# Moving statistics, sums and loads between engines in a 64-graph two-layer GNN kernel

## The reference

```
h = relu(layernorm(x))
q, k, v = h @ Wq.T + bq, h @ Wk.T + bk, h @ Wv.T + bv
p = adj * exp(q @ k.T)
x1 = x + (p / p.sum(axis=2)) @ v                       # layer 0
h1 = relu(layernorm(x1))
hat = adj + eye;  s = hat.sum(-1) ** -0.5
out = x1 + (hat * s[:, None] * s[None, :]) @ (h1 @ W + b)   # layer 1
```

## Time and profile before

| | before |
|---|---|
| median of 3 runs | 1765.69 us (1755.89 to 1776.26) |
| the profiled execution | 1769.79 us |
| its span in the trace | 1768.0 us |
| TensorE busy | 94% |
| VectorE busy | 90% |
| GpSimd busy | 56% |
| ScalarE busy | 49% |
| granted TensorE clock, mean | 0.991 |

### The profile page before, as it was taken

The page is one execution under the profiler, slowest core; times in us unless marked ns, Lnnn a source line. Parts: engine busy times, 40 slices in busy tenths (PEclk is TensorE's granted clock), DMA queues, the critical chain, the costliest instruction groups (busy, mean ns, idle before and its releaser), DMA issues.

```text
span 1768.0 us, 37337 instructions
## 1 busy us (share of the span) xinstructions
PE 1661.1 (94%) x12010; PEld 1558.4 (88%) x12010; DVE 1583.7 (90%) x3558; ACT 866.5 (49%) x1875; POOL 985.6 (56%) x970
## 2 busy tenths in 40 slices
PE   8899999999999999999999999999999999999997
PEld 6789899898888888899998888988998988998996
DVE  6889999999989989899999989989999999998995
ACT  3545445454544454454454454445544444554542
POOL 2655555556556556556556555555665655665561
PEclk9999999999999999999999999999999999999998
DMA  5454354354454554544544543544544545545530
GB/s 174 102 118 132 91 148 131 91 143 126 102 139 112 119 137 98 136 134 102 135 133 100 137 133 90 146 120 105 142 123 106 139 110 121 139 114 118 139 97 27
DMA packets 494415, 212.66 MB, mean 120 GB/s; under 512 B 402496, under 2 KB 427072, under 8 KB 494400
## 3 DMA queue, kind: packets, MB, share of 16 engines
q1 hardware_dynamic: 492480, 210.89, 47.2%
q10 hardware_dynamic: 1920, 1.58, 0.3%
HBM read 146.28 MB, written 66.13 MB: 120 GB/s over the span
## 4 chain that ended last, share of the span: by engine, by line
DVE 29%; issue 29%; POOL 24%; ACT 14%; PE 3%; POOLq 1%; DMA 1%; ACTq 0%; DVEq 0%; SPq 0%
DVE late L740 7%; POOL hat L313 5%; POOL hat_hi L312 5%; POOL hat_lo L315 5%; POOL ht_sum_lo L300 4%; DVE ht L638 4%; ACT late L430 4%; ACT h_hi L432 4%; DVE z_lo L734 3%; DVE st_x L615 3%; POOL rs L318 2%; ACT ht_hi L478 2%; ACT ht_sum_hi L401 2%; DVE p L747 2%; POOL xb L333 1%
## 5 line engine op out<-in xcount | busy, mean ns | idle before, releaser
L333 POOL TENSOR_TENSOR xb<-xb,bv_row 128x512 f32<-128x512 f32 x128 | 165.8, 1316 | 292.3 <-DMA xb<-in_x_dram 292.3
L300 POOL TENSOR_TENSOR ht_sum_lo<-ht_sum,ht_sum_hi 128x512 fp32r<-128x512 f32 x128 | 194.2, 1537 | 207.6 <-ACT ht_sum_hi L401 207.5
L797 PE MATMUL ps<-ht_hi,m_hi 128*128 128x256 f32 x1024 | 286.2, 279 | 0.6 <-DVE m_lo L523 0.6
L799 PE MATMUL ps<-ht_lo,m_hi 128*128 128x256 f32 x1024 | 285.8, 279 | 0.0
L800 PE MATMUL ps<-ht_hi,m_lo 128*128 128x256 f32 x1024 | 285.6, 279 | 0.0
L797 PE MATMUL ps<-w_hi,z_hi 128*128 128x512 f32 x512 | 209.0, 408 | 50.9 <-DVE z_lo L734 50.8
L406 ACT ACTIVATE g_hi<-ps,u_col 128x256 fp32r<-128x256 f32 x256 | 106.2, 466 | 203.9 <-PE ps L800 203.9
L800 PE MATMUL ps<-w_hi,z_lo 128*128 128x512 f32 x512 | 204.6, 400 | 0.0
L799 PE MATMUL ps<-w_lo,z_hi 128*128 128x512 f32 x512 | 204.3, 399 | 0.0
L797 PEld LDWEIGHTS ps<-ht_hi,m_hi 128*128 128x128 f32 x1024 | 192.5, 188 | 0.7 <-DVE m_lo L523 0.7
L800 PEld LDWEIGHTS ps<-ht_hi,m_lo 128*128 128x128 f32 x1024 | 192.4, 188 | 0.0
(11 more groups left out here) (146 smaller groups left out, 5773.4 us busy)
## 6 DMA issues: line engine op xcount, KB each, us to landing
x_in<-in_x_dram SPq DMA_DIRECT2D x64, 512.0 KB, 6.7
xb<-in_x_dram SPq DMA_DIRECT2D x64, 512.0 KB, 7.4
out_dram<-late SPq DMA_DIRECT2D x128, 256.0 KB, 2.1
h_scratch<-h SPq DMA_DIRECT2D x62, 512.0 KB, 3.8
h_blocks<-h_scratch SPq DMA_DIRECT2D x248, 128.0 KB, 4.8
adj_in<-in_adj_dram SPq DMA_DIRECT2D x64, 256.0 KB, 2.9
adj_blocks<-in_adj_dram SPq DMA_DIRECT2D x256, 64.0 KB, 2.5
dn_row<-dn_scratch SPq DMA_DIRECT2D x64, 128.0 KB, 2.9
```

Source lines behind the costliest of these rows:

```text
L300: pool.tensor_tensor(ht_sum_lo[:, pair], ht_sum[:, pair], ht_sum_hi[:, pair].bitcast(fp32), ALU.subtract).then_inc(ht_sum_lo_ready, 1)
L333: last = pool.tensor_tensor(xb[:, t, :], xb[:, t, :], bv_row[:], ALU.add)
L797: pe.matmul(dst, a_hi[:, c, cols], b_hi[:, c, :], start=(first and c == 0), stop=False, skip_group_check=not first)
L799: pe.matmul(dst, a_hi[:, c, cols], b_lo[:, c, :], start=False, stop=False, skip_group_check=not first)
```

## The change

- The statistics of x move from VectorE to ScalarE: `x_sums` (a Copy with an accumulated sum) and `x_squares` (Square with the negative mean as bias, also accumulated). VectorE keeps three short instructions for them: `x_mean`, `x_variance`, `x_shift`.
- `hat` goes. GpSimd adds the 128x128 identity in place to the two diagonal blocks of `adjt`, ScalarE copies `adjt` to `hat_hi`, and GpSimd makes `hat_lo`. The transposed adjacency of the next graph now waits for `hat_lo`.
- GpSimd's order is new: `ht_sums_low` follows `hat_lo` and stands before `rs_1`; `ht_sums` of the next graph follows `dn`, before `rs_x`; the bias goes to `xb` last. ScalarE rounds the sums between its two `e` instead of after `ht_hi`.
- `x_in` and `xb` are loaded by ScalarE on its own queue: `x_in` after `hat_hi`, `xb` after `h1`.
- On VectorE, `transpose_h` comes earlier (after `g_low(1)`), the two `x1b` instructions go between and behind the two `h1_lo`, the statistics of each half of `x1` follow that half at once, and `d` is made by `tensor_scalar` instead of a copy.

```diff
 # SyncE, step
-                if second:
-                    x_second = x_flat[bass.ds(sp.snap((this + 1) * (N * D)), N * D)]
...
-                    sp.dma_start(x_in[:], x_second.rearrange("(t p d) -> p t d", p=P, d=D)).then_inc(x_loaded, 16)
-                if main and prev:
...
-                    sp.dma_start(xb[:], x_this.rearrange("(t p d) -> p t d", p=P, d=D)).then_inc(xb_loaded, 16)
 # GpSimd, step
-                    pool.wait_ge(p_lo_ready[1], this - 1)
+                    pool.wait_ge(p_ready[1], this - 1)
                     if main:
                         pool.wait_ge(ht_lo_ready[1], this)
+                    for t in range(NT):
+                        diagonal = adjt[:, t, t * P:(t + 1) * P]
+                        last = pool.tensor_tensor(diagonal, diagonal, ident[:], ALU.add)
+                    last.then_inc(hat_ready, 1)
+                    pool.wait_ge(hat_hi_ready, this - 1)
                     if older:
                         pool.wait_ge(z_done[1], this - 2)
-                    pool.tensor_tensor(hat_hi[:], adjt[:], eye[:], ALU.add).then_inc(hat_hi_ready, 1)
-                    pool.tensor_tensor(hat[:], adjt[:], eye[:], ALU.add).then_inc(hat_ready, 1)
-                    pool.wait_ge(hat_ready, this - 1)
-                    pool.tensor_tensor(hat_lo[:], hat[:], hat_hi[:].bitcast(fp32), ALU.subtract).then_inc(hat_lo_ready, 1)
-
+                    pool.tensor_tensor(hat_lo[:], adjt[:], hat_hi[:].bitcast(fp32), ALU.subtract).then_inc(hat_lo_ready, 1)
+                    if main:
+                        ht_sums_low(this)
                     pool.wait_ge(ve_1_done, this - 1)
                     pool.tensor_tensor(rs_1[:], ve_1[:], minus_half[:], ALU.pow).then_inc(rs_1_done, 1)
...
-                    pool.wait_ge(xb_loaded, this * 16)
-                    for t in range(NT):
-                        last = pool.tensor_tensor(xb[:, t, :], xb[:, t, :], bv_row[:], ALU.add)
-                    last.then_inc(xb_ready, 1)
...
+                if main and ahead and prev:
+                    pool.wait_ge(v_done[V3], this)
+                    ht_sums(this + 1)
                 if second:
                     pool.wait_ge(ve_x_done, this + 2)
                     pool.tensor_tensor(rs_x[:], ve_x[:], minus_half[:], ALU.pow).then_inc(rs_x_done, 1)
-                if main and ahead:
+                if main:
...
+                    pool.wait_ge(xb_loaded, this * 16)
+                    for t in range(NT):
+                        last = pool.tensor_tensor(xb[:, t, :], xb[:, t, :], bv_row[:], ALU.add)
+                    last.then_inc(xb_ready, 1)
 # ScalarE
+            def load_x(this):
+                x_second = x_flat[bass.ds(act.snap((this + 1) * (N * D)), N * D)]
+                act.wait_ge(h_ready[0], this + 1)
+                act.wait_ge(h_ready[1], this + 1)
+                act.dma_start(x_in[:], x_second.rearrange("(t p d) -> p t d", p=P, d=D)).then_inc(x_loaded, 16)
+
+            def load_xb(this):
+                x_this = x_flat[bass.ds(act.snap((this - 1) * (N * D)), N * D)]
+                act.wait_ge(x1_ready[0], this - 1)
+                act.wait_ge(x1_ready[1], this - 1)
+                act.dma_start(xb[:], x_this.rearrange("(t p d) -> p t d", p=P, d=D)).then_inc(xb_loaded, 16)
...
+            def x_sums(graph):
+                act.wait_ge(x_loaded, graph * 16)
+                for t in range(NT):
+                    last = act.activation(unused_x[:, t, :], x_in[:, t, :], ACT.Copy, accum_out=x_sum[:, t:t + 1])
+                last.then_inc(x_sum_ready, 1)
+
+            def x_squares(graph):
+
+                act.wait_ge(neg_mean_ready, graph)
+                for t in range(NT):
+                    last = act.activation(unused_x[:, t, :], x_in[:, t, :], ACT.Square, bias=neg_mean[:, t:t + 1],
+                                          accum_out=x_square[:, t:t + 1])
+                last.then_inc(x_square_ready, 1)
+
+            def hat_high(this):
+                act.wait_ge(hat_ready, this)
+                act.activation(hat_hi[:], adjt[:], ACT.Copy).then_inc(hat_hi_ready, 1)
 # ScalarE, step
                 if main and ahead:
                     layer_norm_x(this, prev, older)
+                if prev:
+                    if older:
+                        act.wait_ge(z_done[1], this - 2)
+                    hat_high(this - 1)
+                if main and second:
+                    load_x(this)
...
+                if main and prev:
+                    load_xb(this)
                 if main:
                     keep_p1(this)
                     g_high(1, this)
                     keep_p5(this)
+                    if second:
+                        x_sums(this + 2)
                     act.wait_ge(v_done[V2], this)
                     act.activation(v_hi[:, 0, 0, 0:HD], ps[:, VA, 0:HD], ACT.Copy).then_inc(v_hi_ready[0], 1)
+                    if second:
+                        x_squares(this + 2)
...
                     for t in range(NT):
+                        if ahead and prev and t:
+                            ht_sums_high(this + 1)
                         act.wait_ge(s_done[t], this)
...
-                    ht_sums_high(this + 1)
+                    if not prev:
+                        ht_sums_high(this + 1)
 # VectorE
-            def statistics(graph, first=None, second=None):
...
-                    last = dve.bn_stats(st_x[:, t, :], x_in[:, t, :])
...
-                    last = dve.bn_aggr(mv_x[:, t, :], st_x[:, t, :])
...
+            def x_mean(graph):
+                dve.wait_ge(x_sum_ready, graph)
+                dve.tensor_scalar(neg_mean[:], x_sum[:], -1.0 / D, None, ALU.mult).then_inc(neg_mean_ready, 1)
+
+            def x_variance(graph):
+                dve.wait_ge(x_square_ready, graph)
+                dve.tensor_scalar(ve_x[:], x_square[:], 1.0 / D, EPS, ALU.mult, ALU.add).then_inc(ve_x_done, 1)
+
+            def x_shift(graph):
                 dve.wait_ge(rs_x_done, graph)
...
+                dve.tensor_tensor(nb_x[:], neg_mean[:], rs_x[:], ALU.mult).then_inc(ln_x_ready, 1)
 # VectorE, step
-                    dve.tensor_copy(d[:], dn[:]).then_inc(d_ready, 1)
+                    dve.tensor_scalar(d[:], dn[:], 1.0, None, ALU.mult).then_inc(d_ready, 1)
...
+                        if t == 0:
+                            add_bias(0, this - 1)
...
                 if main:
                     value_u2(this)
+                if prev:
+                    add_bias(1, this - 1)
+                if main:
                     g_low(1, this)
+                if prev and ahead:
+                    transpose_h(this)
...
                 if main:
+                    value_u3(this)
                     if second:
-                        statistics(this + 2, lambda: value_u3(this), lambda: value_sums(this))
-                    else:
-                        value_u3(this)
-                        value_sums(this)
+                        x_mean(this + 2)
+                    value_sums(this)
                     value_low(this)
-                if prev and ahead:
-                    transpose_h(this)
+                    if second:
+                        x_variance(this + 2)
...
-                    for t in range(NT):
-                        dve.scalar_tensor_tensor(x1b[:, t, :], b_row[:], sd[:, t:t + 1], x1[:, t, :],
-                                                 ALU.mult, ALU.add).then_inc(x1b_ready[t], 1)
                 if main:
                     value_low_lower(this)
+                    if second:
+                        x_shift(this + 2)
```

More of the change, by code:

```diff
@@ L775, in step @@
                         wt_low()
-                        statistics(this + 2)
+                        x_mean(this + 2)
+                        x_variance(this + 2)
+                        x_shift(this + 2)
                     elif not prev:
```

74 lines of the change are left out of this document (31 added, 43 removed).

## The result

| | before | after |
|---|---|---|
| median of 4 runs each | 1763.25 us (1755.89 to 1776.26) | 1804.39 us (1803.73 to 1806.19) |
| ratio, 95% interval | | 1.0227 [1.0164, 1.0289] |
| span of the profiled execution | 1768.0 us | 1802.5 us |
| mean graph in the loop | 26.80 us | 27.31 us |

The account below looks back on a forecast made before the run. TensorE was taken to bound the loop: 24.95 us plus stalls, 25.25 a graph against 26.80. So 1768.0 - 94.5 + 1.5 = 1675, with 1.8 us beyond the span 1677 us; range 1655 to 1735.

Parts of the forecast that it names:

- TensorE's 24.95 us: TensorE's own matmuls per graph, 19.4 + 5.6 us, claimed as the floor that no order on other engines gets below.
- rival A: TensorE bounds the loop: graphs of 24.95 to 25.6 us, 1658 to 1698 us, own range from 1655; chance 0.62.
- the forecast 21.5 to 23: VectorE's work per graph after the change, in us, down from 23.94 and under TensorE's 24.95 us.
- the `v_p1` stall: TensorE's wait for ScalarE's `v_p1`, 0.5 us a graph before, expected between 0 and 0.6 us.
- The start: Before the loop, ScalarE gets 3 us more and VectorE 2 less: +1.5 us, bounds -1 and +4.
- GpSimd's 5.9 us ahead of `rs_1`: GpSimd's path from the end of `ht_lo` to `rs_1`, claimed level with VectorE's 5.5 us within half a microsecond.
- the length of the DRAM loop: Store of h, reload, transposes and on to the next h: 24.0 us, only 1 us shorter than TensorE's 24.95 us.
- rival B: Transposes of h wait for blocks landing 1 to 2.2 us late: graphs of 25.6 to 26.6, 1698 to 1759 us; chance 0.2.
- The wait for the load holds up nobody any more: With `xb` last on GpSimd, its late load no longer delays `rs_x` and VectorE: graphs from 26.80 to 25.95 us.
- the 0.85 us: Time per graph above the old order's 25.95 us floor, laid to the late `xb` and expected to go entirely.
- Rival C: ScalarE becomes the link everything passes, with two table loads a graph: 27.5 us a graph, 1814 us; chance 0.08.
- Rival D: `x_shift` still waits for `rs_x`, behind GpSimd's four sums: 26.3 to 26.9 us a graph, 1740 to 1777 us; chance 0.1.

Follow-up runs that it names:

- the one run whose blocks are not h's: Changed kernel with the transposes' blocks read from input x of graph 0, issued ahead of SyncE's wait for h: 1666.3 us, one run.
- old places: Changed kernel with transposes of h, GpSimd's `xb` and `rs_x`, and ScalarE's rounding of the sums back in the old order: 1659.37 us, 0.9333.
- `xb` early: Changed kernel with GpSimd adding the bias to `xb` ahead of the four sums of `ht` instead of last: 1764.44 us, 0.9919 of the kernel before.
- `xb` early, store by ScalarE: Changed kernel with the bias added to `xb` ahead of GpSimd's sums and h stored by ScalarE right behind h: 1658.17 us, 0.9325.
- the early transposes alone: The old places kernel with only VectorE's transposes of h put ahead of `v_u3` again, as in the change: 1756.30 us, 0.9951.
- transposes late, rs_x first: Changed kernel with transposes of h back ahead of `z_lo` and GpSimd's `rs_x` ahead of its four sums, `xb` still last: 1720.81 us, 0.9757.
- before, with xb last: Kernel before the change, with only GpSimd's bias addition to `xb` moved behind `rs_x` and the four sums of `ht`: 1863.19 us, 1.0526.
- x late: Changed kernel with ScalarE loading `x_in` together with `xb` after `h1` instead of after `hat_hi`: 1909.83 us, 1.0761.

## Why the prediction was wrong

The direction was wrong, by one step of the working. Point by point:

- **TensorE's 24.95 us** as the floor was right: three kernels reach 24.9 to 25.04 (the last is the one run whose blocks are not h's). So was the worth of the parts that make engines lighter: with the old places the change gives 1659 us, near the 1655 end of rival A's range, and VectorE's work there is 22.6 us a graph (45.28 / 2), within the forecast 21.5 to 23. In the changed kernel it is 23.5 (46.95 / 2), outside. `ht_lo` is 1.29 us a pair as forecast, the `v_p1` stall is 5.3 us in all, and GpSimd's wait for `xb` is short (3.1 us in all, 292.3 before).
- **The start**: 3.0 us for a forecast 1.5, within its bounds.
- **GpSimd's 5.9 us ahead of `rs_1`**: 6.1 (905.40 + 1.29 to 912.82), and level with VectorE, which it waits for by 0.46.
- **The step that failed is the length of the DRAM loop**: "24.0 us. That closes a loop only 1 us shorter than TensorE's 24.95". It is 27.3. Against the estimate, the way from h to its store is 2.3 instead of 0.4 (I took the issue alone, and not what SyncE has in front of it). The store until the block loads is 5.2 instead of 3.8 (the figure of before, taken over although `x_in` had been moved beside it). Transposes to h are 12.95 instead of 11.8, mostly by `v_lo` and `nb_x` beside `xb`: with `xb` early they are 11.50. From the block issue on it is 6.8 instead of 8.0, the one term on the safe side. Together that is 3.3 us more. SyncE's lag could be read off the old trace: its row in the table has 2.37. I saw the mechanism, gave it 0.2 as rival B and priced its landing 1 to 2.2 us late, so even B ended 0.7 us a graph short.
- **"The wait for the load holds up nobody any more"** is true, and the 0.85 us that hung on it still did not come. That the wait was worth 0.85 us is not shown either: two kernels run at TensorE's pace with GpSimd waiting 290.6 us (`xb` early, store by ScalarE) and 223.6 us (old places, `rs_x` behind `xb` as before) for this load, and in the kernel before `nb_x` waited for `rs_x` 15.9 us in all. The prediction freed `xb` from its place and asked who waits for its result. What lies beside it was charged to VectorE's total work, with 0.5 to 2 us, and not to the path from the transposes to h. On the kernel before, that place alone costs 5.3%.
- **Rival C** had the sign but not the mechanism: one table load in the whole execution, and TensorE waits for ScalarE less than before. **Rival D** is real, and hidden as long as the loop of rival B is longer; it shows once the transposes are late.

## What to carry to other kernels

When an order changes, add up the closed loops that pass through a DMA, and take each leg from issue to issue, with what the issuing queue has to wait for in front of it, not from landing times. A move that starts a consumer earlier is worth nothing if its producer is the end of such a loop: the slack that looked like waste was what absorbed the transfer (here the early transposes alone cost 6%). And a long wait is no proof of a cost: the 290 us wait for `xb` stood in the fastest kernel too. And when work on GpSimd moves, look at both sides: who waits for its result, and which VectorE instructions will lie beside it, since even an instruction as small as `nb_x` (0.15 us) took 1.25 us beside one.

## What the runs showed of the hardware

- A VectorE instruction on 128x2 with two inputs in SBUF took 0.15 us by itself and 1.25 beside a GpSimd addition on 128x512 (`nb_x`, `xb` early and the changed kernel); a 0.48 us one took 1.51 (transposes late, rs_x first), and a pair of 0.75 took 2.95 (before, with xb last).
- The store of 512 KB landed in 3.0 to 3.8 us where it was issued ahead of the loads of x, and in 5.2 with one load of 512 KB issued 1.9 us ahead on another queue. The four block loads of 128 KB went from 4.1 to 6.9 us with 1 MB started beside them (x late).
- Two Copies of 128x512 with an accumulated sum follow each other at 0.61 us and two Squares at 0.72, with their 0.2 us reads partly hidden; Square, Copy, Relu and Exp came with one table load of 1.28 us in the execution.
